# Scores two groups further ahead of the values, output weights split in the context stage, and one running maximum in PSUM

## The reference

```
q, k, v  = LN(x) @ wq, @ wk, @ wv            # 16 query heads, 4 key/value heads, 128 wide
k_ctx, v_ctx = ctx @ wk_ctx, @ wv_ctx        # 4096 rows
q, k, k_ctx = rms_norm per head;  q, k rotated
scores = q . [k_ctx, k] / sqrt(128) + causal mask on the own part
out    = softmax(scores) . [v_ctx, v]        # 16 heads
x      = x + out.reshape(256, 2048) @ wo     # wo is 2048 x 512
```

## Time and profile before

| | |
|---|---|
| median of 3 runs | 995.39 us (993.46 to 995.46) |
| profiled execution | 996.27 us, of which its span 994.5 us |
| mean granted TensorE clock | 0.997 of full speed |
| PE busy | 973.3 us (98% of the span) |
| DVE, ACT, POOL busy | 784.6 (79%), 612.4 (62%), 560.9 us (56%) |
| DMA | 131.10 MB, 132 GB/s on average |

### The profile page before, as it was taken

How to read it: one execution, slowest core, us unless ns; L and a number is a source line. 1 busy time by engine, 2 the same in 40 slices (tenths; PEclk the granted TensorE clock), 3 DMA queues, 4 the chain that set the end, 5 groups by cost and what they waited for, 6 DMA issues and landing times.

```text
span 994.5 us, 15791 instructions
## 1 busy us (share of the span) xinstructions
PE 973.3 (98%) x5695; PEld 857.6 (86%) x5695; DVE 784.6 (79%) x1178; ACT 612.4 (62%) x1026; POOL 560.9 (56%) x517
## 2 busy tenths in 40 slices
PE   8999999999889999999999999988999999999998
PEld 7888888889779999999999999976788988888887
DVE  6754667645988888888888898899798887777775
ACT  5443343336656777767667767774488666666663
POOL 3543444331579999999999999997001032222222
PEclk9999999999999999999999999999999999999999
DMA  8557654566202221141204032220610685555540
GB/s 289 160 184 251 212 189 128 169 227 219 105 1 87 95 75 32 44 138 46 62 1 146 36 111 109 75 95 1 235 62 1 243 310 197 189 189 188 190 159 22
DMA packets 56525, 131.10 MB, mean 132 GB/s; under 512 B 4192, under 2 KB 36352, under 8 KB 55424
## 3 DMA queue, kind: packets, MB, share of 16 engines
q1 hardware_dynamic: 56448, 130.09, 38.7%
HBM read 101.21 MB, written 28.87 MB: 131 GB/s over the span
## 4 chain that ended last, share of the span: by engine, by line
PE 90%; DVE 4%; POOL 3%; issue 2%; ACT 1%; DMA 1%; SPq 0%; DVEq 0%; POOLq 0%; ACTq 0%
PE bank L526 18%; PE bank L629 17%; PE bank L600 17%; PE bank L508 13%; PE bank L928 9%; PE bank L930 5%; POOL first_max L1918 2%; PE bank L736 1%; PE bank L535 1%; DVE first_max L1093 1%; PE bank L623 1%; PE bank L625 1%; PE bank L627 1%; DVE first_max L1085 1%; PE bank L792 1%
## 5 line engine op out<-in xcount | busy, mean ns | idle before, releaser
L600 PE MATMUL bank<-qT_hi,kT 128*128 128x256 f32 (+1 forms) x1088 | 296.0, 346 | 1.7 <-DVE first_max L1089 1.4
L1918 POOL TENSOR_TENSOR first_max<-first_max,weights 128x512 f32<-128x512 f32 x214 | 280.7, 1312 | 18.9 <-ACT weights L1627 1.0
L629 PE MATMUL bank<-weights,vN 128*128 128x256 f32 (+1 forms) x896 | 260.7, 378 | 0.0
L1623 ACT COPY weights<-bank 128x512 f32<-128x512 f32 (+1 forms) x272 | 154.8, 580 | 100.9 <-PE bank L600 61.6
L600 PEld LDWEIGHTS bank<-qT_hi,kT 128*128 128x128 f32 x1088 | 196.9, 190 | 20.7 <-issue 1.6
L1093 DVE TENSOR_TENSOR first_max<-bank,first_max 128x512 f32<-128x512 f32 x196 | 134.8, 688 | 36.7 <-ACT weights L1623 31.6
L1114 DVE TENSOR_TENSOR weights<-weights,bank 128x1024 f32<-128x1024 f32 x128 | 154.8, 1210 | 1.8 <-PE bank L656 1.8
L1627 ACT ACTIVATE weights<-weights 128x1024 f32<-128x1024 f32 x144 | 144.5, 1003 | 17.8 <-DVE weights L1114 17.7
L600 PE MATMUL bank<-qT_lo,kT 128*128 128x256 f32 (+1 forms) x544 | 153.8, 283 | 0.0
L526 PE MATMUL bank<-w_ctx_hi,ctx_hl 128*128 128x512 f32 x512 | 144.3, 393 | 1.4 <-ACT w_ctx_hi L1586 1.4
L629 PEld LDWEIGHTS bank<-weights,vN 128*128 128x128 f32 x896 | 142.7, 190 | 3.3
(11 more groups left out here) (258 smaller groups left out, 1735.0 us busy)
## 6 DMA issues: line engine op xcount, KB each, us to landing
e_raw<-in_experts SPq DMA_DIRECT2D x51, 768.0 KB, 4.4
k_spill<-k_stage SPq DMA_DIRECT2D x16, 1024.0 KB, 5.6
kT<-k_spill SPq DMA_DIRECT2D x15, 1024.0 KB, 5.3
v_spill<-v_stage SPq DMA_DIRECT2D x16, 512.0 KB, 6.7
vN<-v_spill SPq DMA_DIRECT2D x16, 512.0 KB, 3.6
ctx_raw<-in_ctx SPq DMA_DIRECT2D x15, 512.0 KB, 4.0
w_raw<-in_w_qkv SPq DMA_DIRECT2D x6, 1024.0 KB, 5.1
comb<-c_spill SPq DMA_DIRECT2D x8, 512.0 KB, 5.7
```

Source lines behind the costliest of these rows:

```text
L600: done = e.matmul(dst, kT[:, w, kt * P:(kt + 1) * P], qT[a][:, h, q0:L], start=m == 0, stop=m == 2)
L629: done = e.matmul(dst[:, q0:L], vN[:, kt, :], weights[:, cols], start=kt == 0, stop=kt == KTILES - 1)
L1623: e.copy(s_buf[h % 2][:, g, 0:width(g)], bank[SCORE_BANKS[s % len(SCORE_BANKS)]][:, 0:width(g)]).then_inc(taken, 1)
L1918: e.tensor_tensor(run_sum[:, :], run_sum[:, :], here, ALU.add).then_inc(summed, 1)
```

## The change

Six things, all in one edit.

1. `LEAD` goes from 29 to 31. All work on weights (subtract, exponential, sums, values) moves two steps later against the scores. `TURN_AT`, `REDUCE_AT` and `SPREAD_AT` get an entry of their own for head 1 (5, 5, 7); heads 2 to 14 keep 4, 5, 6.
2. Head 1 keeps its running maximum in the PSUM bank that the values of odd heads use later, no longer in memory next to the scores. The fold of head 0, one reduction over 1024 columns, becomes two maxima of 512 and 256 columns.
3. `wo` is split in the context stage, in 32 chunks of 128x256 (128 KB), one per iteration: SP loads the chunk, ACT casts its main part at the iteration's end, POOL takes the rest in the next iteration, SP writes both to memory (`wo_parts`). There are two buffers for chunks and one for main parts, so ACT's cast of chunk `c` waits until both parts of chunk `c - 1` have arrived in memory.
4. In the tail the 16 casts and 16 subtractions of `wo` go; SP loads the rests where it loaded `wo`, and the main parts by four transfers of 1 MB behind the loop.
5. POOL adds the first 2 groups of head 15 instead of the first 6; DVE adds the others.
6. POOL takes the rest of a split group's weights one step earlier; the projection's main parts start 3 steps later and its rests 1 step later.

The diff, cut to its core:

```diff
-LEAD = NG + 12
+LEAD = NG + 14
 SUB_AHEAD, EXP_AHEAD = 6, 4
-TURN_AT, REDUCE_AT, SPREAD_AT = (5, 4, 2), (2, 5, 3), (7, 6, 3)
+TURN_AT, REDUCE_AT, SPREAD_AT = (5, 5, 4, 2), (2, 5, 5, 3), (7, 7, 6, 3)
-OWN_SUMS = 6
+OWN_SUMS = 2
-WO_CASTS, WO_MAIN, WO_LOWS, WO_REST = 241, 243, 246, 249
+WO_MAIN, WO_REST = 246, 250
+WC = DM // 2
+NWC = NH * DM // WC
...
+        wo_parts = nc.dram_tensor("wo_parts", (2, P, NH, DM), F32).ap()
+        wo_chunk = [back.take(f"wo_chunk{i}", [WC]) for i in range(2)]
+        wo_main = back.take("wo_main", [WC], F32R)
...
+            def maxima_of(h):
+                return bank[VALUE_BANKS[1]] if h == 1 else run_max
...
             def fold_max(h):
...
+                if h == 0:
+                    e.tensor_tensor(first_max[:, 0, :], first_max[:, 0, :], first_max[:, 1, :], ALU.max).then_inc(maxed, 1)
+                    dve.wait_ge(maxed, plan.folded[0] - 1)
+                    e.tensor_tensor(both_max[:, :], first_max[:, 0, 0:L], first_max[:, 0, L:2 * L], ALU.max).then_inc(maxed, 1)
+                    return
...
-            def rest_of_wo(i):
-                h = WO_ORDER[i]
-                dve.wait_ge(wo_hi_done, i + 1)
-                e.tensor_tensor(wo_lo[:, h, :], wo_sb[:, h, :], wo_hi[:, h, :], ALU.subtract).then_inc(wo_lo_done, 1)
...
+            def main_of_wo(c):
+                act.wait_ge(wo_chunk_in, 16 * (c + 1))
+                act.wait_ge(wo_parts_out, 32 * c)
+                e.copy(wo_main[:, :], wo_chunk[c % 2][:, :]).then_inc(wo_hi_done, 1)
...
+                main_of_wo(i)
...
+            def rest_of_wo(c):
+                pool.wait_ge(wo_hi_done, c + 1)
+                e.tensor_tensor(wo_chunk[c % 2][:, :].bitcast(F32R), wo_chunk[c % 2][:, :], wo_main[:, :], ALU.subtract).then_inc(wo_lo_done, 1)
...
             for n in range(NH * NG):
-                if n % NG in SPLITS:
-                    rest_of_weights(n)
+                if (n + 1) % NG in SPLITS:
+                    rest_of_weights(n + 1)
...
+            def load_wo(c):
+                h, cols = wo_columns(c)
+                if c >= 2:
+                    sp.wait_ge(wo_parts_out, 32 * (c - 1))
+                e.dma_start(wo_chunk[c % 2][:, :], t["wo"][:, h, cols]).then_inc(wo_chunk_in, 16)
+
+            def spill_wo(c):
+                h, cols = wo_columns(c)
+                sp.wait_ge(wo_hi_done, c + 1)
+                e.dma_start(wo_parts[0][:, h, cols], wo_main[:, :].bitcast(F32)).then_inc(wo_parts_out, 16)
+                sp.wait_ge(wo_lo_done, c + 1)
+                e.dma_start(wo_parts[1][:, h, cols], wo_chunk[c % 2][:, :]).then_inc(wo_parts_out, 16)
+
             for i in range(NT):
                 if (i + 1) % BT == BT - 1 and i + 1 < NT:
                     load_ctx((i + 1) // BT + NCR)
+                load_wo(i)
+                if i:
+                    spill_wo(i - 1)
                 if i >= 1 and (i - 1) % BT == BT - 1:
                     spill((i - 1) // BT)
...
+            for j in range(NH // 4):
+                sp.wait_ge(pv, NG * (H15 - 1) + 4 * j + 4)
+                sp.wait_ge(summed, summed_at(H15 - 1, 4 * j + 3))
+                e.dma_start(wo_hi[:, 4 * j:4 * j + 4, :].bitcast(F32), wo_parts[0][:, 4 * j:4 * j + 4]).then_inc(wo_hi_in[j], 16)
```

More of the change, by code:

```diff
@@ L128, in __init__ @@
             if s % NG == NG - 1:
-                done += 1
+                done += 1 if h else 2
                 self.folded.append(done)
@@ L683, in project_rest @@
                 h = WO_ORDER[i]
-                pe.wait_ge(wo_lo_done, i + 1)
+                load = [any(lo <= h < hi for lo, hi in part) for part in WO_LOADS].index(True)
+                pe.wait_ge(*(wo_in[load], 48) if load < KD else (w_xb_in, 32))
                 done = e.matmul(bank[tt][:, :], outT[0][:, h, tt * P:(tt + 1) * P], wo_lo[:, h, :], start=False, stop=i == NH - 1)
@@ L699, in pe_program @@
                 if h in range(NH):
-                    if k == TURN_AT[(h > 0) + (h == H15)]:
+                    if k == TURN_AT[(h > 0) + (h > 1) + (h == H15)]:
                         turn_max(h)
-                    if k == SPREAD_AT[(h > 0) + (h == H15)]:
+                    if k == SPREAD_AT[(h > 0) + (h > 1) + (h == H15)]:
                         spread_max(h)
@@ L1088, in running_max @@
                     dve.wait_ge(maxed, plan.folded[h - 1])
-                    e.tensor_tensor(run_max[:, :], here[:, :], slot[:, plan.groups[s - 1][1], :], ALU.max).then_inc(maxed, 1)
+                    e.tensor_tensor(top[:, :], here[:, :], slot[:, plan.groups[s - 1][1], :], ALU.max).then_inc(maxed, 1)
                 elif s % NG:
@@ L1182, in dve_program @@
                 h, k = divmod(s - NG, NG)
-                if k == REDUCE_AT[(h > 0) + (h == H15)] and h in range(NH):
+                if k == REDUCE_AT[(h > 0) + (h > 1) + (h == H15)] and h in range(NH):
                     reduce_rows(h)
@@ L1638, in finish_head @@
                 e.copy(outT[0][:, h, :], head_out[h % 2][:, :]).then_inc(oT_hi, 1)
-            def main_of_wo(i):
-                h = WO_ORDER[i]
-                load = [any(lo <= h < hi for lo, hi in part) for part in WO_LOADS].index(True)
-                act.wait_ge(*(wo_in[load], 48) if load < KD else (w_xb_in, 32))
-                act.wait_ge(pv, NG * (H15 - 1) + h + 1)
-                act.wait_ge(summed, summed_at(H15 - 1, h))
-                e.copy(wo_hi[:, h, :], wo_sb[:, h, :]).then_inc(wo_hi_done, 1)
             for s in range(NH * NG + LEAD):
```

42 lines of the change are left out of this document (24 added, 18 removed).

## The result

| | before | changed |
|---|---|---|
| median | 994.97 us (993.46 to 995.46, 4 runs) | 1026.94 us (1025.38 to 1027.54, 4 runs) |
| span of the profiled execution | 994.5 us | 1023.3 us |
| PE, DVE, ACT, POOL busy | 973.3, 784.6, 612.4, 560.9 | 980.9, 764.9, 617.1, 573.2 |

The ratio is 1.032, with an interval from 1.030 to 1.034: slower, by twice what the prediction said, and outside its range of 991 to 1020.

A forecast was written before the change was run, and what follows sets the result against it. PE, working 98% of the span, was taken to bound the kernel. Terms 5.0 + 5.7 + 0.5 + 1.7 − 8.0 + 15.6 − 4.5 = +16.0 us gave a forecast of 1012 us, range 991 to 1020.

The forecast's parts named there:

- A: Start of the context stage: ACT's cast of `wo` chunk 0 delays the split of context tile 2, +5.0 us.
- the rival of the queue: Context stage: small transfers don't queue behind large ones, so 12.9 us of loss go, giving 999.4; chance 0.13.
- B: Key loads at 210 us +5.7 us, hand-over to the scores +0.5, halved clock behind the stall +1.7.
- The step that failed: Context stage up to iteration 25: ACT's stalls cost nothing, since ACT has room and PE's own projections cover them.
- C: Ramp, 252 to 283 us: head 1's maxima, moved to PSUM, take 690 ns; −8.0 us, bounds −10 and −3.
- The two parts that I set against each other: Ramp: head 1's maxima end 8 us earlier, but 1.7 is lost since two values fewer lie there: −6.3.
- D: Heads 2 to 14: PE's spread waits 1.2 us per head for the last subtraction; 13 heads give +15.6 us.
- my two times: Steady heads: the chain to the spread ends at 422.7, or 423.3 if ACT's cast comes first; PE waits 0.7 to 1.25.
- The first rival: Steady heads: DVE reaches the last subtraction in time, so the spread's wait goes, giving 992.4; chance 0.17.
- E: Tail: waits for `wo` and weights' rests go, −6.7 us with clock, but the last spread adds +2.2; −4.5 in all.

## Why the prediction was wrong

**A, the start: the delay of ACT right, the sum a little small, PE's path another.** Chunk 0 landed at 20.3 (issued 14.02, 6.3 us) and the split of tile 2 began at 20.67, as worked out. The turn of tile 3 stands 6.7 us late (47.12 against 40.46) for my 5.0. But PE did not lose this by a late split of tile 3, as I had it. It waited 1.0 for the split of tile 2 (at 21.42) and then, for the most part, for VectorE:

```profile
30.10 0.86 PE L546 MATMUL bank<-ident,k_normed 128*128 128x128 f32 x4 [2.56 <-DVE k_normed L1029]
```

VectorE had stood still 5.2 us for ACT's late cast of own weights (until 23.12), and made the rest of those weights before it came to these keys. Behind this wait the granted clock was 0.57 from 30 to 34 us, a price that I had put on the key loads alone. That the sum comes within 1.7 us is so in part luck.

The chunk of 14.02 landed 0.3 us after the context load issued before it (13.65, 6.4 us). So the small transfer does stand behind the large one, and the rival of the queue fell. The Trainium skill, page "DMA: Bandwidth & Descriptors", section "Queues, rings and completion order", says that each DMA engine takes descriptors in ring order, though a later transfer may finish its write before an earlier one. The first half agrees with this landing. The second half agrees with two transfers of the changed kernel: the chunk load of 49.98 landed at 57.7, and the main part issued behind it, at 50.45, had landed at 55.9:

```profile
wo_chunk<-in_wo SPq DMA_DIRECT2D x1, 128.0 KB, 7.7
wo_parts<-wo_main SPq DMA_DIRECT2D x1, 128.0 KB, 5.5
```

Both were late all the same, so this freedom did not help the kernel.

**B, the key loads and hand-over: right.** The tiles slip another 7.2 us there (from 19.3 to 26.6) for 5.7, 0.5 and 1.7. The wait is 5.6 and the rest of the slip stands with the slow clock behind it; the 0.5 of the hand-over is not seen, since the first scores are as late as the last turn before them (26.6).

**The step that failed** is the sentence between them: "From there to iteration 25 ACT has room ... so I cost its stalls at nothing". It cost 12.7 us: 4.9 at 59 us, 2.4 at 93, 2.1 at 125, 2.7 at 157 (each the growth of the distance between the turns of the two kernels) and 0.6 from 178 to 194. I had set ACT's busy time, 83 of 210 us, against the added casts. A wait is not busy time: ACT stood 64.5 us before chunk casts that themselves take 0.4 each. The runs show where the cost came from: with one chunk instead of 32 it is gone, and with all 32 and an iteration more for each it is gone as well. The question to ask was how long a chunk's transfers take where the queue is fullest, and how many tiles PE has in reserve at that time; I had worked with exactly that at 14 and at 210 us. I looked at two meetings of large and small transfers and not at those of every fourth iteration.

**C, the ramp: right.** −7.6 for −8.0. Maxima in PSUM took 693 ns for my 690; putting that maximum back took the gain away. PE's waits in the ramp were 8.7 us by my own rows, not the 10 that I wrote beside the sum. The two parts that I set against each other were both there: the maxima and the fold alone bring 8.7 us (75.7 to 67.0), and with LEAD at 31 it is 7.6.

The Trainium skill, page "VectorE: DVE Perf Modes", section "The TRN2 errata — SBUF-src ops pay a fixed extra latency per instruction", would have the form that reads a bank the slower one. No run here shows that: the forms agree within 5 ns, 688 with the scores in a bank, 693 with the maximum in one, and 690 with both inputs in memory while POOL did nothing.

**D, the steady heads: right.** 13 × 1.03 = 13.4 for 15.6, each head's chain 5.8 us as worked out; it starts near the early one of my two times, so the wait is 0.86. The first rival, that VectorE comes in time, fell.

**E, the tail: right in kind.** −3.7 for −4.5 (the −2.7 of the table without 1.03 of its spread). The waits for `wo` and for two of the rests went, and the last spread waits 2.5 instead of 1.8. Two sizes were wrong here and offset each other: I had that wait grow by 2.2 and it grew by 0.7, and I had 6.7 gained beside it and it was 4.4. That the sum comes near is luck.

In sum 26.6 − 7.6 + 13.4 − 3.7 + 0.1 = 28.8. With term A to iteration 25 at its true size the forecast would have stood 13 us higher, at 1025.

The range was also added up wrongly. With each term at its ends the sum goes from 995 to 1025, not from 1003 to 1020. The measured 1026.9 lies above that too, as the term that failed stood at nothing and had no bounds.

## What to carry to other kernels

When a step with a transfer is put into a pipeline, compare the transfer's time at its fullest place in the queue with the slack that buffers give it, not the engine's busy share with the added work: the same 32 chunks cost 26 us with one buffer for main parts and nothing with an iteration and the buffers for it more. When one number shifts a chain against another, walk through every wait that pairs the two chains and shift its place as well. And try the parts of an edit alone: here one part of six carried most of the gain, and two others hid it (parts 4 to 6 were not tried alone).

## What the runs showed of the hardware

VectorE's maximum over 128x512 with both inputs in memory took 690 ns on average while POOL did nothing (8 of them) and 1277 beside POOL's work (6), and 694 beside POOL with one input and the output in PSUM.

The 128 KB transfers of `wo` took from 1.7 us (a rest issued at 43.57) to 9.2 us (the chunk load of 231.32, between key loads of 1 MB).

A stall of TensorE of 2.7 us was followed by products at the lower clock (granted 0.69 of full speed on average from 60 to 63 us, and 0.50, which is 1.2 GHz, from 62 to 64), just as one of 5.6 was (0.51 from 242 to 245.5). Behind the three of 1.5 to 2.1 us (93, 125 and 157 us) the granted clock stayed at 1.00 (2.4 GHz). So the idle time of the two longest is not their whole price: the turns slipped by 4.9 and 7.2 us.
